# Pole products, cosine products, mask and weight splits in other places around the down products, and the last output unit in two halves

## What is computed

```python
xn = layernorm(x)
x = x + S4(xn) + FFN(xn)           # layer 0
xn = layernorm(x)
x = x + attention(xn) + MoE(xn)    # layer 1
```

```python
at_roots = c * (k00 - k01 * (1.0 / (1.0 + k11)) * k10)   # c, k..: per root of unity
K = jnp.fft.ifft(at_roots, L).real
y = irfft(rfft(u, n=2*L) * rfft(K, n=2*L), n=2*L)[..., :L] + D[0] * u
h = silu(xn @ W_gate.T) * (xn @ W_up.T);  out = h @ W_down.T
```

## Time and profile before

| | |
|---|---|
| median of 3 runs | 1104.12 us (1103.63 to 1104.66) |
| the profiled execution's own time | 1104.64 us |
| its span | 1102.9 us |
| PE busy | 1086.5 us, 99% of the span |
| PE weight loads / DVE / ACT / POOL busy | 87% / 68% / 51% / 67% |
| mean granted TensorE clock | 0.994 |
| HBM | 51.26 MB read, 2.10 MB written, 48 GB/s over the span |

### The profile page before, as it was taken

How to read it: one execution, slowest core, us unless ns; L and a number is a source line. 1 busy time by engine, 2 the same in 40 slices (tenths; PEclk the granted TensorE clock), 3 DMA queues, 4 the chain that set the end, 5 groups by cost and what they waited for, 6 DMA issues and landing times.

```text
span 1102.9 us, 21381 instructions
## 1 busy us (share of the span) xinstructions
PE 1086.5 (99%) x6370; PEld 960.0 (87%) x6370; DVE 745.2 (68%) x1841; ACT 562.3 (51%) x1690; POOL 743.3 (67%) x1030
## 2 busy tenths in 40 slices
PE   9998989999999999999999999999999999999998
PEld 8886867899898899889988988898899889988987
DVE  7598567285776667666676667666666666676675
ACT  4444211133664666456455555554665465545663
POOL 4777458797864993679387739764886479469911
PEclk9999899999999999999999999999999999999999
DMA  5111142200210120012001101110111011101102
GB/s 176 34 58 58 44 141 65 86 34 11 77 40 20 59 77 21 7 54 76 20 19 51 66 19 57 40 39 19 59 39 39 19 59 57 39 10 53 54 1 77
DMA packets 23731, 54.39 MB, mean 49 GB/s; under 512 B 3408, under 2 KB 3728, under 8 KB 23504
## 3 DMA queue, kind: packets, MB, share of 16 engines
q1 hardware_dynamic: 23632, 53.37, 14.8%
HBM read 51.26 MB, written 2.10 MB: 48 GB/s over the span
## 4 chain that ended last, share of the span: by engine, by line
PE 94%; DVE 3%; POOL 1%; DMA 1%; issue 1%; ACT 0%; SPq 0%; POOLq 0%; DVEq 0%; ACTq 0%
PE banks L184 28%; PE banks L185 28%; PE banks L186 28%; PE banks L2067 4%; PE banks L2086 3%; PE banks L2058 3%; PE banks L1176 1%; POOL wd_lo L480 0%; PE banks L1364 0%; DMA acc<-in_x 0%; DMA wd_stage<-in_w_down 0%; DVE s L920 0%; POOL wc_lo L486 0%; POOL wd_hi L478 0%; DVE banks L856 0%
## 5 line engine op out<-in xcount | busy, mean ns | idle before, releaser
L1633 POOL TENSOR_TENSOR form_lo<-wqk_stage,form_hi 128x256 fp32r<-128x256 f32 x192 | 142.2, 741 | 16.0
L1687 POOL TENSOR_SCALAR vf_hi<-wvo_stage 128x512 fp32r<-128x512 f32 (+1 forms) x48 | 26.4, 550 | 166.4 <-PE banks L186 152.9
L1967 ACT ACTIVATE prob<-prob,top 128x128 f32<-128x128 f32 (+1 forms) x256 | 115.6, 460 | 17.0 <-DVE top L1996 16.9
L1973 ACT ACTIVATE prob<-prob,inv 128x128 f32<-128x128 f32 (+1 forms) x256 | 102.7, 451 | 38.4 <-DVE inv L2002 38.4
L1996 DVE CUSTOM_DVE_ANT_0 prob<-banks,mask 128x128 f32<-128x128 f32 (+1 forms) x256 | 81.3, 355 | 59.5 <-PE banks L186 45.3
L2014 DVE TENSOR_TENSOR acc<-acc,banks 128x512 f32<-128x512 f32 x128 | 86.7, 681 | 36.1 <-PE banks L186 36.1
L184 PE MATMUL banks<-tT_hi,form_hi 128*128 128x512 f32 x256 | 105.6, 412 | 0.0
L185 PE MATMUL banks<-tT_lo,form_hi 128*128 128x512 f32 x256 | 100.2, 391 | 0.0
L186 PE MATMUL banks<-tT_hi,form_lo 128*128 128x512 f32 x256 | 100.1, 391 | 0.0
L184 PE MATMUL banks<-wo_hi,oT_hi 128*128 128x512 f32 x240 | 95.9, 400 | 0.0
L186 PE MATMUL banks<-wo_hi,oT_lo 128*128 128x512 f32 x240 | 93.6, 390 | 0.0
(11 more groups left out here) (351 smaller groups left out, 3736.2 us busy)
## 6 DMA issues: line engine op xcount, KB each, us to landing
wqk_stage<-in_w_qk SPq DMA_DIRECT2D x32, 512.0 KB, 3.2
wvo_stage<-in_w_v SPq DMA_DIRECT2D x34, 256.0 KB, 2.6
wvo_stage<-in_w_o SPq DMA_DIRECT2D x32, 256.0 KB, 2.6
wd_stage<-in_w_down SPq DMA_DIRECT2D x22, 256.0 KB, 2.6
gu_stage<-in_w_gu SPq DMA_DIRECT2D x10, 512.0 KB, 3.3
acc<-in_x SPq DMA_DIRECT2D x8, 256.0 KB, 5.2
out<-acc SPq DMA_DIRECT2D x8, 256.0 KB, 2.0
tab<-in_w_comb SPq DMA_DIRECT2D x1, 1300.0 KB, 5.9
```

Source lines behind the costliest of these rows:

```text
L1633: nc.gpsimd.tensor_tensor(form_lo[:, part], src[:, :], as_f32(form_hi[:, part]), ALU.subtract).then_inc(form_ready, 1)
L1967: ins = nc.scalar.activation(pr, pr, ACT.Exp, bias=top[:, n % 2, r:r + 1], scale=-1.0, accum_out=total[:, n % 2, r:r + 1])
L1973: ins = nc.scalar.activation(pr, pr, ACT.Copy, scale=inv[:, n % 2, r:r + 1])
```

## The change

Six edits. The pole products move from ahead of tile 9 to ahead of tile 10. `roots(0)` moves from after tile 10 to after tile 9. The cosine products move from after down chunk 4 to after down chunk 5 (`TOEP_AFTER` = 6). On SP the loads 9 and 10 move ahead of the linear weights, load 4 to 10 now standing before them. On GpSimd the mask stays between splits 7 and 8, written with the new constant; three pieces of the linear weights are split in a row after split 12, and the fourth after split 21. The output unit of token tile 7 is cut into two halves of 256 columns, each with its own products, signal, add and store.

```diff
@@ LAST
-    ("T", 15), ("W", 2, 1), ("W", 2, 2), ("O", 15), ("E", 15)] + [("W", 2, t) for t in range(TH - 1, NT)]
+    ("T", 15), ("W", 2, 1), ("W", 2, 2), ("O", 15), ("E", 15)] + [("W", 2, t) for t in range(TH - 1, NT - 1)] + [
+    ("W", 2, NT - 1, slice(0, HALF_D)), ("W", 2, NT - 1, slice(HALF_D, DM))]
...
-MASK_AFTER = 7
+TOEP_AFTER = 6
@@ sync_program of layer0
-        for n in range(4, 9):
+        for n in range(4, NF):
             load_wd(n)

         sp.wait_ge(toep_done, 1)
...
-        for n in range(9, 2 * NF):
+        for n in range(NF, 2 * NF):
             load_wd(n)
@@ gpsimd_program of layer0
-        for n in range(MASK_AFTER + 1):
+        for n in range(TOEP_AFTER + 2):
             split_wd(n)
...
         pool.wait_ge(wc_loaded, 32)
-        split_comb(0)
-        split_comb(1)
-        split_wd(NF + 2)
-        split_comb(2)
-        split_wd(NF + 3)
-        split_comb(3)
-        for n in range(NF + 4, 2 * NF):
+        for k in range(KD - 1):
+            split_comb(k)
+        for n in range(NF + 2, 2 * NF):
             split_wd(n)
+        split_comb(KD - 1)
@@ vector_program of layer0
-        pieces = [small_vectors, cauchy_real, cauchy_imag, cauchy_numerators, cauchy_reciprocal, cauchy_inverse]
+        pieces = [small_vectors, cauchy_real, cauchy_imag, cauchy_numerators, cauchy_reciprocal, cauchy_inverse,
+                  lambda: roots(0)]
         for f in range(ND, NF):
             f_tile(f)
-            if f - ND < len(pieces):
+            if f < NF - 1:
                 pieces[f - ND]()
-        roots(0)
         roots(1)
@@ tensor_program of layer0
-            if f == ND + 6:
+            if f == NF - 1:
...
-        down(0, range(0, 5))
+        down(0, range(0, TOEP_AFTER))
...
-        down(0, range(5, NF))
+        down(0, range(TOEP_AFTER, NF))
@@ attention: tensor_program and vector_program, step "W"
+                        part = w_cols(step)
-                        ins = matmul3(nc, turn_bank(steps, step), left[0][:, k, cols], left[1][:, k, cols],
-                                      right[0][:, k], right[1][:, k], k == 0, k == PAIRED - 1)
+                        ins = matmul3(nc, turn_bank(steps, step)[:, part], left[0][:, k, cols], left[1][:, k, cols],
+                                      right[0][:, k, part], right[1][:, k, part], k == 0, k == PAIRED - 1)
...
-                    nc.vector.tensor_tensor(acc[:, t, :], acc[:, t, :], turn_bank(steps, step),
+                    nc.vector.tensor_tensor(acc[:, t, part], acc[:, t, part], turn_bank(steps, step)[:, part],
                                             ALU.add).then_inc(w_added, 1)
@@ attention: sync_program, the stores
-        for t in range(NT):
-            sp.wait_ge(w_added, w_count(NG - 1, LAST, ("W", 2, t)))
-            sp.dma_start(out[t * P:(t + 1) * P, :], acc[:, t, :]).then_inc(out_done, 16)
+        for step in ends:
+            t, part = step[2], w_cols(step)
+            sp.wait_ge(w_added, w_count(NG - 1, LAST, step))
+            sp.dma_start(out[t * P:(t + 1) * P, part], acc[:, t, part]).then_inc(out_done, 16)
```

More of the change, by code:

```diff
@@ L79 @@
 AHEAD_V = range(BATCH)
+HALF_D = DM // 2
 MIDDLE_SLOTS = [
@@ L512, in gpsimd_program @@
                                 base=0, pattern=[[1, P]], channel_multiplier=-1).then_inc(toep_masked, 1)
-        for n in range(MASK_AFTER + 1, NF + 2):
+        for n in range(TOEP_AFTER + 2, NF + 2):
             split_wd(n)
         pool.wait_ge(wc_loaded, 32)
-        split_comb(0)
-        split_comb(1)
-        split_wd(NF + 2)
-        split_comb(2)
-        split_wd(NF + 3)
-        split_comb(3)
-        for n in range(NF + 4, 2 * NF):
+        for k in range(KD - 1):
+            split_comb(k)
+        for n in range(NF + 2, 2 * NF):
             split_wd(n)
+        split_comb(KD - 1)
         nc.gpsimd.tensor_scalar(wb_hi[:, :], wb_stage, 1.0, 1.0, ALU.mult, ALU.mult).then_inc(comb_hi_done, 1)
@@ L1486, in w_count, with w_cols @@
         return before + adds(steps).index(step) + 1
+    def w_cols(step):
+        return step[3] if len(step) > 3 else slice(0, DM)
     def value_products(g, steps, j, i):
@@ L1592, in sync_program @@
         groups(sp, group)
-        for t in range(NT):
-            sp.wait_ge(w_added, w_count(NG - 1, LAST, ("W", 2, t)))
-            sp.dma_start(out[t * P:(t + 1) * P, :], acc[:, t, :]).then_inc(out_done, 16)
-        sp.wait_ge(out_done, 16 * NT)
+        ends = [step for step in LAST if step[0:2] == ("W", 2)]
+        for step in ends:
+            t, part = step[2], w_cols(step)
+            sp.wait_ge(w_added, w_count(NG - 1, LAST, step))
+            sp.dma_start(out[t * P:(t + 1) * P, part], acc[:, t, part]).then_inc(out_done, 16)
+        sp.wait_ge(out_done, 16 * len(ends))
     def prepare(pool, g, h, part):
@@ L2011, in group @@
                 elif kind == "W":
-                    t = step[2]
+                    t, part = step[2], w_cols(step)
                     dve.wait_ge(w_done, w_count(g, steps, step))
-                    nc.vector.tensor_tensor(acc[:, t, :], acc[:, t, :], turn_bank(steps, step),
+                    nc.vector.tensor_tensor(acc[:, t, part], acc[:, t, part], turn_bank(steps, step)[:, part],
                                             ALU.add).then_inc(w_added, 1)
```

## The result

| | before | after |
|---|---|---|
| median of four runs | 1104.39 us (1103.63 to 1104.82) | 1087.70 us (1087.31 to 1088.49) |
| profiled execution, own time | 1104.64 us | 1087.31 us |
| its span | 1102.9 us | 1085.5 us |
| its mean granted clock | 0.994 | 1.000 |

The ratio is 0.9851, 95% interval [0.9833, 0.9868]: 16.7 us less by the medians, where 16.6 were forecast. The time of 1087.7 stands beside the 1087.5 predicted.

A forecast was written before the change was run, and what follows sets the result against it. TensorE was taken to bound the kernel. Terms 9.1 + 4.8 + 2.6 - 0.4 + 0.5 = 16.6 us, off 1104.64, gave 1088.0, or 1087.5 us on the median's footing; range 1084.8 to 1092.0.

The forecast's parts named there:

- poles: Between tiles 8 and 10: pole products one tile later end a 10.9 us interruption, cost 1.75, gain 9.1 us.
- cosine products: After six down chunks: the wait for the phases goes (3.1 us) and the half clock too (1.7), gain 4.8 us.
- splits and loads: Down and linear weights on SP and GpSimd: one wait of some 1.1 us replaces three, gain 2.6 us.
- fourth linear piece: Split after split 21, it makes GpSimd 2.45 us later at the linear stage's mixes, costing 0.4 us.
- halves: Last output unit in two halves: shorter last add and smaller last transfer, gain 0.5 us.
- the step that looked for a second wait behind this one: Tile 9, rival of chance 0.04: another wait behind the pole wait cuts that gain to 4 us, 1092.5.
- roots(0): On VectorE after tile 9: runs 116.4 to 120.6, hidden; U3 there at 122.7, asked for at 125.25.
- Load 11 therefore lands near 150.6 + 8.5 = 159.1: Down weight load queued on SP behind linear weights and wb: lands 8.5 us after the linear weights' issue at 150.6.
- no wait at chunk 13: Rival, chance 0.10: back-to-back transfers cost their bytes alone, split 13 is in time at chunk 13, 1086.4 us.
- the first rival: Linear weights become the wait: TensorE stands 2.6 to 5 us at chunk 13, 1089 to 1093, chance 0.17.
- VectorE as the bound in tile 10: Rival, chance 0.07: roots(0) long or late, TensorE stands 1 to 3 us before the down products, 1089 to 1092.
- a time above 1104: Rival "slower", chance 0.02: load 11 landing after 170.6 delays every later split; 14 us late gives 1106.6.

The follow-up runs named there:

- e2: Changed kernel with the cosine products back after five down chunks instead of six: 1087.96 us.
- e3: Changed kernel with roots(0) back behind tile 10, cosine products still after six down chunks: 1088.29 us.
- e4: Changed kernel with both put back, roots(0) behind tile 10 and the cosine products after five down chunks: 1091.86 us.
- e5: Changed kernel with down weight loads 9 and 10 back behind the linear weights on SP: 1089.08 us.
- e7: Changed kernel with the fourth piece of the linear weights split ahead of split 19 instead of after split 21: 1087.91 us.
- e10: Changed kernel with the fourth linear piece ahead of split 19 and the last output unit cut at column 384 instead of 256: 1087.81 us.
- e11: The changed kernel itself measured once more, with no edit: 1088.28 us.
- e9: Kernel before with one part alone, the pole products moved one tile later: 1095.74 us.
- e1: Changed kernel with the pole products back ahead of tile 9, all else kept: 1096.49 us.

## Why the prediction was right, step by step

| term | predicted | from the traces | undone, or alone |
|---|---|---|---|
| poles | 9.1 (7.4 to 10.0) | 8.8 | 8.8, 8.5 |
| cosine products | 4.8 (3.1 to 5.1) | 4.9 | 4.2 |
| splits and loads | 2.6 (0.5 to 3.8) | 3.1 | 2.8 (with the fourth piece), 1.4 |
| fourth linear piece | -0.4 (0 to -1.5) | -0.5 | -0.5 (trace alone) |
| halves | 0.5 (0 to 0.7) | 0.5 | 0.7, 0.2 (medians); 0.5 (trace) |
| sum | 16.6 | 16.8 | |

The traces' sum is 0.1 over the 16.7 between the spans, with the start-up taken out. That the forecast came within 0.2 us of it is in part luck: the poles were put 0.3 too high and the splits and loads 0.5 too low, and the two errors cancel. Nor can medians tell 0.2 us apart here.

**Poles.** The rule "what a wait gives back, the end gets" held, and the step that looked for a second wait behind this one was right to find none. The interruption was 10.9 us and is now 115.22 - 113.02 - 0.23 = 1.97 us and 0.1 for the slower first matmul. The products' price at the full clock, the one value without a row, was taken at half of 3.51, 1.75. From the first of them to the next tile's first matmul, as the 3.51 was counted, it is 1.88 (113.34 to 115.22), a little over half; 0.09 us more pass before the first one starts. That is 0.2 of the 0.3 us by which the term was too large, and the slower first matmul the rest. They begin at 113.34; forecast was 113.96 less the start-up's 0.70.

**roots(0).** Forecast to run 4.24 us and to put U3 2.5 us ahead of TensorE's question; it took 4.9 (from 115.54 to tile 10's P2 at 120.41), U3 was there at 122.5 and tile 10 ended at 124.98: 2.5. Hidden as argued.

**Cosine products.** From the end of the chunk ahead to the slot of the next one's second matmul it was 156.54 - 148.02 - 0.23 = 8.29 us and is 144.97 - 141.31 - 0.23 = 3.43. The slack was forecast at 4.1 us and is 5.2 (136.1 to 141.3). What the prediction did not say, and e2 and e3 showed, is that the change holds two remedies for one wait: with roots(0) ahead of tile 10 the sixth chunk is reserve only, with the sixth chunk 0.2 us is left without roots(0). e4 gives the wait's whole price. Its first run, with no half clock, is 3.1 us over the changed kernel's 1087.7, the other three 3.8 to 4.8: the term's two cases, without the half clock and with it, both occur.

**Splits and loads.** This is the mis-sized term. The step that failed is "Load 11 therefore lands near 150.6 + 8.5 = 159.1" and with it "one wait of some 1.1 us". Counted from the end of chunk 5 (T0, forecast 141.6, now 141.31) the forecast had the linear weights' issue at +9.0, load 11 at +17.5, split 13 done at +31.0 and chunk 13 ready at +29.9. Measured: 9.3, 16.8 (158.12), 30.4 (171.71) and, with small delays at chunks 8 and 10 that no step had, about 30.2. TensorE stood 171.76 - 171.33 - 0.23 = 0.20 us and lost 0.1 to a slow start. The landing was 7.5 us behind the issue of the linear weights and not 8.5, since wb's time to landing, taken over from the earlier trace rows as 7.3, was 6.2. The DMA issues of 104 to 210 us, KB and us to landing, of the changed kernel and then of e5:

```profile
tab<-in_w_comb SPq DMA_DIRECT2D x1, 1300.0 KB, 6.0
...
tab<-in_w_expb SPq DMA_DIRECT2D x1, 256.0 KB, 6.2
```

```profile
tab<-in_w_comb SPq DMA_DIRECT2D x1, 1300.0 KB, 5.8
tab<-in_w_expb SPq DMA_DIRECT2D x1, 256.0 KB, 6.0
```

Of the rivals, "no wait at chunk 13" described this better than the forecast did. The delays at chunks 8 and 10 cost 0.17 us each. They are waits on splits too, too short for the list of waits: splits 8 and 10 end at 150.21 and 155.92, the chunks start at 150.26 and 155.98, 0.06 and 0.07 us after their slots, and slowly. Both splits took 2.4 us instead of 2.0 (low parts of 1.60 and 1.71 us where 1.29 is the median). These two delays stand in e7's, e10's and e11's traces as well; that at chunk 13 is in e11's and missing in e7's and e10's. So the gain is 3.8 - 0.3 - 0.34 = 3.2. Read directly, from the matmul behind the cosine products to the transposes, it is 43.68 us before (156.54 to 200.22) less one chunk of 2.72, and 37.84 now (144.97 to 182.81): 3.1. The rule of the Trainium skill (DMA: Bandwidth & Descriptors, Anatomy of one DMA) had load 11 at 157.2, 6.6 us behind that issue: the measured 7.5 is halfway between it and the 8.5 from the rows.

**Fourth piece.** The term was the right size: 0.27 us of wait, 0.16 that the wait doesn't count and a first matmul 0.07 slower. It was cost without need: e7 shows that 2.49 us of GpSimd's idle time lay nearer by.

**Halves.** As forecast: the add fell from 0.69 to 0.42, and 2.73 us remain from the last matmul's slot to the end where 3.29 were, less 0.07 for the stream. Of its parts, the smaller transfer gave less than the 0.4 us worked out by the slope of the loads: from the end of the last add to the span's end it is 2.1 us for 2.4. e10 shows the limit of going on that way.

**Slips in the working.** The half clock around the cosine products is 3.5 us in the first part and 3.4 in the third. A gain of 3.8 instead of 2.6 would make the sum 17.8 and not 17.7. The range ends at 1092.0, while the first rival, which it is said to take in, goes to 1093. None of these decides anything here.

The rivals of a new wait at chunk 13 over 2 us, of VectorE as the bound in tile 10, and of a time above 1104 left no trace: nothing in tiles 9 and 10 waits, and the longest new wait is 0.3 us.

## What to carry to other kernels

When an engine stands for a result of a slower one, look first whether its consumer can be asked for one tile later: here moving sixteen small matmuls behind 42 large ones gave 8.8 us for a wait of 4.8, since the granted clock went with the wait. Where two moves serve one wait, undo both together as well as one by one; singly each looked worth nothing here, and together they were worth 4.2 us. Before giving a queue a new order, lay the pieces into its idle times: the same piece cost 0.5 us at the end of GpSimd's row and nothing in a gap ten microseconds ahead.

## What the runs showed that was not expected

A wait of the same length brings the half clock in some executions and not in others: 2.91 us in the trace of e4 did not, 2.92 us in those of before and of e9 did. The runs' mean granted clocks say the same, though the waits of the runs without a trace are not known. With the poles moved alone (e9) the wait of 2.92 us stayed, and three runs had 0.998 (1095.57 to 1096.12) and one 1.000 (1094.18). In e4, with a wait of 2.91 us, again three had 0.998 and one 1.000 (1090.84, the others 1091.51 to 1092.53). The kernel before doesn't repeat exactly either: of the nine runs beside e9 five had 0.994 (1104.25 to 1105.74 us) and four 0.995 (1103.52 to 1104.01); in which of its two stretches they differ isn't on record. The fall, where it comes, costs 1.7 us in the cosine products. TensorE had been busy without a pause for over 25 us ahead of the wait in both kernels; what decides between the two outcomes stays open. The wait of 4.8 us had the half level behind it in the trace of before and in that of e1; one other run of e1 had 0.997 where three had 0.995, so less time at the half level, and took 1096.08 us where the traced one took 1096.22.

A store's time to landing hardly depends on its size at this end of the scale: 2.0 us for 256 KB, 1.8 for 192 and 128 KB, 1.7 for 64 KB. Here the last store's end was brought forward by an earlier add and little by a smaller store.
